# A tile table with 16 segments in the second round; the results of the first seven batches combined during the expert tiles

## The reference

```
h = layernorm(x) * (1 + ca) + sa
x = x + ga * mixer(h)
h = layernorm(x) * (1 + cb) + sb
x = x + gb * moe(h)
```

## Time and profile before

| what | value |
|---|---|
| median of 3 runs | 648.27 us (644.71 to 653.47) |
| the profiled execution | 647.95 us, span 645.8 us |
| busy share of the span | PE 84%, PEld 64%, DVE 75%, ACT 64%, POOL 53% |
| first tile's first layer starts, last tile's | 250.0 us, 587.7 us |
| end stage: first load issued, last ScalarE copy starts | 605.4 us, 642.5 us |
| DMA | 52.23 MB, mean 81 GB/s |

### The profile page before, as it was taken

The page is one execution under the profiler, slowest core; times in us unless marked ns, Lnnn a source line. Parts: engine busy times, 40 slices in busy tenths (PEclk is TensorE's granted clock), DMA queues, the critical chain, the costliest instruction groups (busy, mean ns, idle before and its releaser), DMA issues. The chain is left out here.

```text
span 645.8 us, 15964 instructions
## 1 busy us (share of the span) xinstructions
PE 542.2 (84%) x3102; PEld 411.9 (64%) x3103; DVE 486.6 (75%) x2313; ACT 416.5 (64%) x1126; POOL 341.6 (53%) x442
## 2 busy tenths in 40 slices
PE   2889878886878526978999999999999999997097
PEld 1445444444445414966898888898888898896042
DVE  5989667777577626756898888898888888889187
ACT  0457546555555213756788788888787887887386
POOL 3552656666465654255655655655555656566300
PEclk9999887888888655988999999999999999999589
DMA  6944111111111213121111111111111211110498
GB/s 182 306 151 105 47 41 39 46 42 42 34 47 42 73 39 115 51 55 47 54 58 52 55 53 53 57 53 53 55 51 53 57 47 56 49 51 34 153 369 267
DMA packets 60169, 52.23 MB, mean 81 GB/s; under 512 B 8902, under 2 KB 53177, under 8 KB 60006
## 3 DMA queue, kind: packets, MB, share of 16 engines
q1 hardware_dynamic: 51718, 34.92, 19.5%
q0 software_dynamic: 8416, 16.93, 7.3%
HBM read 29.67 MB, written 22.58 MB: 81 GB/s over the span
## 5 line engine op out<-in xcount | busy, mean ns | idle before, releaser
L493 POOL DMA_INDIRECT expert_rows<-rows,slot x128 | 124.1, 969 | 94.0 <-issue 49.7
L521 POOL DMA_INDIRECT expert_results<-y,target x135 | 134.0, 993 | 49.5 <-issue 48.6
L1190 PE MATMUL bank<-W,h2T 128*128 x1080 | 144.0, 277 | 1.0 <-ACT h2T L626 0.8
L1190 PEld LDWEIGHTS bank<-W,h2T 128*128 128x128 f32 x1080 | 132.4, 193 | 1.7 <-issue 1.7
L618 ACT ACTIVATE h1T<-bank 128x512 f32<-128x512 f32 x135 | 80.4, 596 | 55.4 <-PE bank L1177 49.9
L1006 DVE BATCH_NORM_STATS2 stf<-h1T 128x6 f32<-128x512 f32 x135 | 91.0, 674 | 0.0
L984 DVE SCALAR_TENSOR_TENSOR wmod<-bank,rse,c 128x128 f32<-128x128 f32 x135 | 47.4, 351 | 56.0 <-issue 29.2
L1181 PE MATMUL bank<-ident,h1T 128*128 128x128 f32 x540 | 82.3, 275 | 1.7 <-ACT h1T L618 1.7
L1181 PEld LDWEIGHTS bank<-ident,h1T 128*128 128x128 f32 x540 | 68.4, 143 | 21.4 <-ACT h1T L618 2.5
L626 ACT ACTIVATE h2T<-bank 128x512 f32<-128x512 f32 x135 | 79.1, 586 | 0.3 <-PE bank L1181 0.3
L1174 PE MATMUL bank<-b_parts,onesr 128*128 x135 | 66.1, 489 | 5.5 <-DVE h3lo L998 3.6
(11 more groups left out here) (203 smaller groups left out, 1106.7 us busy)
## 6 DMA issues: line engine op xcount, KB each, us to landing
hrow<-expert_rows SPq DMA_DIRECT2D x135, 65.0 KB
X<-in_L_attn_x SPq DMA_DIRECT2D x8, 512.0 KB, 7.4
W<-expert_results SPq DMA_DIRECT2D x8, 512.0 KB, 6.4
out_x<-X SPq DMA_DIRECT2D x16, 256.0 KB, 5.3
expert_results<-y,target POOLq DMA_INDIRECT x135
expert_rows<-rows,slot POOLq DMA_INDIRECT x128
xi<-expert_results SPq DMA_DIRECT2D x4, 512.0 KB, 7.2
b_parts<-expert_results SPq DMA_DIRECT2D x4, 512.0 KB, 7.5
```

Source lines behind the costliest of these rows:

```text
L493: nc.gpsimd.indirect_dma_start(out=rows_d, out_offset=bass.IndirectOffsetOnAxis(ap=slot[q][:, n // TOPK, n % TOPK:n % TOPK + 1], axis=0), ...
L521: nc.gpsimd.indirect_dma_start(out=results_d, out_offset=bass.IndirectOffsetOnAxis(ap=target[n % TURN][:], axis=0), in_=y[k][:], in_offset ...
L1190: ins = mm(acc, rT[q][:, ch * P:(ch + 1) * P], W2[:, bass.ds(e2 * CF + ch, 1), :], start=(ch == 0), stop=(ch == CF - 1))
```

## The change

- ROUND1_BATCHES is 7 instead of 10, so the first round has 48 tiles and the second 87.
- The second round's table has 16 segments instead of 8: first, per expert, the tiles that still hold rows of the first seven batches, then, per expert, all others. The vectors of the table (nt_f, ends, jump, past, hop) are 16 wide; begin_row holds each segment's first row, jump the step between segments. After tile 63 all results of batches 0 to 6 are computed.
- EARLY = 7 batches are combined during the expert tiles, batch b in turn 10 + b (steps 80 to 135). SP loads its results into the two buffers xi (load_early) behind the loads of that turn's tiles, and stores batch b two turns later (store_early). ScalarE does one of its four gate copies at the end of steps n = 3 to 6 (early_y0g), VectorE one of its four sums at the end of steps n = 4 to 7 (early_sum). GpSimd, not VectorE and TensorE, multiplies with gb (ahead of the turn's second tile) and adds to X (ahead of its fifth), both 128x512.
- The early gates are 0.5 + 0.5 tanh(d / 2), from a Tanh ahead of the first Sqrt and two operations of VectorE in step 4. The Sigmoid of the other nine batches stays behind the tiles.
- The loops of turns end at turn 10 on SP, GpSimd, ScalarE and VectorE; turns 10 to 15 are unrolled there. TensorE keeps its loop to turn 16.
- The end stage has nine batches, unrolled on all engines; per batch it does what it did.

```
-    ROUND1_BATCHES = 10
+    ROUND1_BATCHES = 7
...
+        EARLY = ROUND1_BATCHES
+        EARLY_TURN = (ROUND1 + TOPK * E - 1) // 8 + 3
+        early01 = [t[:].rearrange("p c l -> p (c l)").rearrange("p (j k) -> p j k", j=J) for t in xi]
+        early_gb = [t[:, :].rearrange("p (j d) -> p j d", j=J) for t in scan]
...
             peeled(TURN, LOOP2[0])
-            with engine.Fori(LOOP2[0] // TURN, LOOP2[1] // TURN) as turn:
+            with engine.Fori(LOOP2[0] // TURN, loop_end // TURN) as turn:
                 loaded = load(turn * TURN + oldest, TURN + 2)
                 for n in range(TURN):
                     step(turn * TURN + n, n, lambda k: loaded[k - oldest + n])
+            for begin in range(loop_end, LOOP2[1], TURN):
+                peeled(begin, begin + TURN)
             peeled(LOOP2[1], LAST2 + 1)
+
+        def early_batch(s):
+
+            b = s // TURN - EARLY_TURN if isinstance(s, int) else -1
+            return b if 0 <= b < EARLY else None
...
+            def results_of(tiles_stored):
+                for n in range(RESULTS):
+                    sp.wait_ge(results_stored[n], 16 * ((tiles_stored + RESULTS - 1 - n) // RESULTS))
+
+            def load_early(b):
+                if b == 0:
+                    results_of(ROUND1 + TOPK * E - 1)
+                if b >= 2:
+                    sp.wait_ge(early_sum_ready, b - 1)
+                sp.dma_start(early01[b % 2], results_v[:, tiles(b), :]).then_inc(early_loaded[b % 2], 16)
+
+            def store_early(b):
+                sp.wait_ge(early_out_ready, b + 1)
+                sp.dma_start(out_v[:, tiles(b), :], X[:, tiles(b), :]).then_inc(out_stored, 16)
+
+            with sp.Fori(ROUND1 // SLOTS, EARLY_TURN) as turn:
                 for n in range(SLOTS):
                     load_next(turn * SLOTS + n, n)
-            for i in range(EXPERT_TILES // SLOTS * SLOTS, EXPERT_TILES):
-                load_next(i, i % SLOTS)
-
-            for n in range(RESULTS):
-                sp.wait_ge(results_stored[n], 16 * ((EXPERT_TILES + RESULTS - 1 - n) // RESULTS))
+            for turn in range(EARLY_TURN, EARLY_TURN + EARLY + 2):
+                for i in range(turn * SLOTS, min((turn + 1) * SLOTS, EXPERT_TILES)):
+                    load_next(i, i % SLOTS)
+                if turn - EARLY_TURN < EARLY:
+                    load_early(turn - EARLY_TURN)
+                if turn - EARLY_TURN >= 2:
+                    store_early(turn - EARLY_TURN - 2)
+
+            results_of(EXPERT_TILES)
...
+            sp.wait_ge(early_sum_ready, EARLY)
             for n in range(Y_SLOTS):
-                load_results(n, n)
-            with sp.Fori(1, B // Y_SLOTS) as turn:
-                for n in range(Y_SLOTS):
-                    b = turn * Y_SLOTS + n
-                    sp.wait_ge(ysum_ready, b - Y_SLOTS + 1)
-                    load_results(b, n)
-                    store_out(b - Y_SLOTS)
-            for n in range(Y_SLOTS):
-                store_out(B - Y_SLOTS + n)
+                load_results(EARLY + n, n)
+            for m in range(B - EARLY):
+                if m + Y_SLOTS < B - EARLY:
+                    sp.wait_ge(ysum_ready, m + 1)
+                    load_results(EARLY + m + Y_SLOTS, m)
+                store_out(EARLY + m)
...
+            def early_gb_of(b):
+                pool.wait_ge(early_sum_ready, b + 1)
+                if b == 0:
+                    pool.wait_ge(gb_loaded, 16)
+                if b >= 2:
+                    pool.wait_ge(early_out_ready, b - 1)
+                nc.gpsimd.tensor_tensor(early_gb[b % 2], ysum[b % 2][:], gb_rows[:, b:b + 1, :].broadcast_to([P, J, D]),
+                                        ALU.mult).then_inc(early_gb_ready, 1)
+
+            def early_out_of(b):
+                pool.wait_ge(early_gb_ready, b + 1)
+                nc.gpsimd.tensor_tensor(X[:, tiles(b), :], X[:, tiles(b), :], early_gb[b % 2], ALU.add).then_inc(early_out_ready, 1)
+
             def turn_of_results(turn, count, first):
                 _, expert = nc.values_load_multi_w_load_instructions(
                     pool_experts[0:1, bass.ds(turn * TURN, count)], engines=(mybir.EngineType.Pool,), min_val=0,
                     max_val=E - 1, skip_runtime_bounds_check_because="a count of experts, cut off at E - 1")
+                b = early_batch(turn * TURN)
                 for n in range(count):
+                    if b is not None and n == 1:
+                        early_gb_of(b)
+                    if b is not None and n == 4:
+                        early_out_of(b)
...
+            with pool.Fori(1, EARLY_TURN) as turn:
+                turn_of_results(turn, TURN, False)
...
+            act.wait_ge(ids_ready, EARLY)
+            nc.scalar.activation(gate[:, 0, 0:EARLY * J], lead[:, 0:EARLY * J], ACT.Tanh, scale=0.5).then_inc(half_gate_ready, 1)
             nc.scalar.activation(root_of_eps[:], eps[:], ACT.Sqrt)
+
+            def early_y0g(b, j):
+                if b == 0 and j == 0:
+                    act.wait_ge(early_gates_ready, 1)
+                if j == 0:
+                    act.wait_ge(early_loaded[b % 2], b // 2 * 16 + 16)
+                    if b >= 2:
+                        act.wait_ge(early_sum_ready, b - 1)
+                nc.scalar.activation(y0g[b % 2][:, j, :], early01[b % 2][:, j, 0:D], ACT.Copy,
+                                     scale=gate[:, 0, b * J + j:b * J + j + 1]).then_inc(early_y0g_ready, 1)
...
+                b = early_batch(s)
+                if b is not None and 3 <= n < 3 + J:
+                    early_y0g(b, n - 3)
+
+            run_tiles(act, expert_step, loop_end=EARLY_TURN * TURN)
...
+                if parts > E:
+                    vec.tensor_scalar(own_turn[:], own_e[:], float(E), -float(E), ALU.is_ge, ALU.mult)
+                    link(vec.tensor_tensor(own_row[:], own_row[:], begin_row[:, 0:1], ALU.add))
+                    link(vec.tensor_tensor(own_e[:], own_e[:], own_turn[:], ALU.add))
...
+                old, new = slice(0, E), slice(E, EE)
                 dve.wait_ge(count_done, 1)
                 vec.tensor_copy(cnt_i[:], bank[5][:, 0:E]).then_inc(counts_ready, 1)
-                link(vec.tensor_scalar(cnt[:], bank[5][:, 0:E], float(P - 1), None, ALU.add))
+                vec.tensor_scalar(cnt[:, old], cnt1_i[:], float(P - 1), None, ALU.add)
+                link(vec.tensor_scalar(cnt[:, new], bank[5][:, 0:E], float(P - 1), None, ALU.add))
                 link(vec.tensor_copy(nt_i[:], cnt[:]))
                 link(vec.tensor_scalar(nt_i[:], nt_i[:], P.bit_length() - 1, None, ALU.logical_shift_right))
                 link(vec.tensor_copy(full[:], nt_i[:]))
-                vec.tensor_tensor(past[:], done1[:, 1:E + 1], done1[:, 0:E], ALU.subtract)
-                link(vec.tensor_tensor(nt_f[:], full[:], done1[:, 0:E], ALU.subtract))
-                link(vec.tensor_tensor(past[:], past[:], nt_f[:], ALU.subtract))
-                link(vec.tensor_scalar(jump[:], past[:], float(P), float(REGION), ALU.mult, ALU.add))
-                spread_table(done1[:, 0:1])
+                vec.scalar_tensor_tensor(begin_row[:, old], done1[:], float(P), base_e[:], ALU.mult, ALU.add)
+                vec.tensor_tensor(nt_f[:, old], full[:, old], done1[:], ALU.subtract)
+                vec.tensor_tensor(nt_f[:, new], full[:, new], full[:, old], ALU.subtract)
+                link(vec.scalar_tensor_tensor(begin_row[:, new], full[:, old], float(P), base_e[:], ALU.mult, ALU.add))
+                link(vec.tensor_tensor(step_of[:], begin_row[:, 1:EE + 1], begin_row[:, 0:EE], ALU.subtract))
+                link(vec.scalar_tensor_tensor(jump[:], nt_f[:], -float(P), step_of[:], ALU.mult, ALU.add))
+                spread_table(EE)
...
+                b = early_batch(s)
+                if b is not None and 4 <= n < 4 + J:
+                    early_sum(b, n - 4)
...
+                if isinstance(s, int) and s == 4:
+                    early_gates()
...
+            def early_gates():
+                part = slice(0, EARLY * J)
+                dve.wait_ge(half_gate_ready, 1)
+                vec.tensor_scalar(gate[:, 1, part], gate[:, 0, part], -0.5, 0.5, ALU.mult, ALU.add)
+                vec.tensor_scalar(gate[:, 0, part], gate[:, 0, part], 0.5, 0.5, ALU.mult, ALU.add).then_inc(early_gates_ready, 1)
+
+            def early_sum(b, j):
+                dve.wait_ge(early_y0g_ready, b * J + j + 1)
+                if b >= 2 and j == 0:
+                    dve.wait_ge(early_gb_ready, b - 1)
+                ins = vec.scalar_tensor_tensor(ysum[b % 2][:, j, :], early01[b % 2][:, j, D:2 * D],
+                                               gate[:, 1, b * J + j:b * J + j + 1], y0g[b % 2][:, j, :], ALU.mult, ALU.add)
+                if j == J - 1:
+                    ins.then_inc(early_sum_ready, 1)
+
+            run_tiles(dve, expert_step, mybir.EngineType.DVE, dve_experts, -5, EARLY_TURN * TURN)
...
+            def sums(m):
```

(4 more changed lines are left out.)

150 lines of the change are left out of this document (71 added, 79 removed).

## The result

The changed kernel takes 666.81 us (median of 4 runs, 664.65 to 671.08) against 646.49 (4 runs, 644.28 to 653.47) beside it: a ratio of **1.029, 95% interval 1.020 to 1.038**. It is slower, at the edge of 2% by the interval, where 650.5 and "within 2%" were predicted, and 4.8 us above the range. The profiled execution took 664.65 us, span 662.8. (In all that follows medians take every execution of a kernel; ratios leave out those more than 1.5% above its fastest.)

What follows compares the result with a forecast made beforehand. TensorE was taken as the bound, full in the expert tiles with VectorE close behind, and again in the end stage. 647.95 - 12.2 + 3.5 + 7.0 + 4.4 = 650.65, stated as 650.5 us; range 638.5 to 662.

Steps and rivals of the forecast that it cites:

- part 5: The rest (first table's move, Tanh gates, 16 segments, early stores, GpSimd's other operations): put at nothing.
- part 3: Turns 10 to 15: ScalarE waits for the late early load, delaying h3hi, h3lo and TensorE; 7.0 us more (0 to 10).
- Part 1: End stage: seven batches leave it at 1.74 us each, 12.2 us less, TensorE staying the bound.
- Part 2: Last tiles: the seventh early batch adds two 128x512 GpSimd operations of about 1.25 us; 3.5 us more (1.5 to 5).
- Part 4: Early-work turns: VectorE's four sums and the turn boundary, with GpSimd's multiplication, delay TensorE; 4.4 us more (0 to 9).
- lock in full: Rival, early-work turns: each of GpSimd's two operations holds VectorE 1.25 us, 10.5 us more, so 661; chance 0.08.
- hidden: Rival, expert tiles: early work is hidden, load and VectorE costs shrink to 0 to 3 us, 639.3 to 642; chance 0.29.
- Straight-line pauses: Rival, six unrolled turns: one VectorE pause each, 18.6 us with some 5 overlapping other stalls, so 664; chance 0.14.
- The end saves less: Rival, end stage: nine batches run at 2.2 us rather than 1.74, 4 us back, 654.5; chance 0.05.

Runs made afterwards that it cites:

- e13: The changed kernel unchanged, run a third time, on one of the later chips: 591.70 us, 1.010 of the kernel before.
- e2: The changed kernel with each early load issued behind its turn's second tile load, six tile loads earlier: 650.29 us, 0.999 of the kernel before.
- e17: The changed kernel with GpSimd's 128x512 operations cut into four 128x128 ones each, early loads left late: 588.85 us, 1.004 of the kernel before.
- e9: The changed kernel with six early batches, loads six tile loads earlier, first table at the tenth batch, GpSimd's operations in 128x128 pieces: 573.36 us, 0.977 of before.
- e5: The changed kernel unchanged, run once more on the second chip: 663.42 us, 1.023 of the kernel before.
- e3: The kernel before with turns 10 to 15 unrolled on SP, GpSimd, ScalarE and VectorE, no early work: 650.75 us, 0.999 of the kernel before.
- e16: The same kernel as e9, run again on another later chip: 573.72 us, 0.979 of the kernel before.
- e6: The changed kernel with six early batches, loads six tile loads earlier, first table at the tenth batch, GpSimd's operations whole: 643.03 us, 0.989 of before.
- e1: The kernel before with ROUND1_BATCHES = 7 alone, no early work: 656.04 us, 1.011 of the kernel before.
- e14: As e9, but with the first table at the seventh batch as in the changed kernel: 574.65 us, 0.980 of the kernel before.

## Why the prediction was wrong

Predicted was +2.7 us, measured +17.0 in the spans: 14.3 us to find. Two steps failed. The larger is in part 5, "the first table moves from one mixer step to another at the same cost": it was put at nothing, and 11.0 us went ahead of tile 16. The other is the stall of part 3 in the turns behind the first, taken as 1.25 us a turn and measured as 2.13, with a fall of TensorE's clock on top for which no part had a term. On a chip of the later kind, where the first costs nothing, the changed kernel is 5.7 us slower than before (e13) with +2.7 predicted; that this is so near is in part luck, since the end stage, better than summed, pays for some of the stalls.

- **Part 1 (end, -12.2): right.** 1.72 us a batch against 1.74. The stage as a whole is 13.5 shorter (40.4 to 26.9): the first load landed in 3.62 instead of 4.03 us, and the second batch's matmuls ran at the full clock, 0.86 us in the chain where before it was 1.46.
- **Part 2 (GpSimd's tail, +3.5): right in place, a third too high.** The estimate of 1.25 us for 128x512 was 1.30; the last addition came 2.35 us later relative to tile 134. Part of the tail showed up as TensorE's wait in turn 16 instead. End and tail together gave -11.2 where -8.7 was summed, 2.5 too pessimistic.
- **Part 3 (early load, +7.0): mechanism right, mis-sized.** The step named (load behind the eighth tile load, ScalarE, h3hi, h3lo, TensorE) is what rows and e2 show. The first turn was right: 3.22 less 2.38 = 0.84 against 0.7. The five later ones took 2.13 on average (4.15, 4.90, 4.24, 4.66, 4.58 at tile n = 5, less 2.38) against 1.25. Of the 0.9 missing, some 0.45 is the issue, 1.0 later than in the first turn where I had 0.55: the target that releases it is held by GpSimd's addition. With short operations (e17) 0.4 of that 1.0 is still there. Some 0.25 is the landing (4.06 from issue to copy on average, 3.8 taken; in four of the five turns a store of 256 KB goes out beside the load). This stall alone is 11.5 us.
- **Part 4 (VectorE, +4.4): size nearly right, cause wrong.** It was put on the four sums and the turn's boundary (0.65 each). With the load ahead the stretch costs 3.3 (134.0 less 130.7), and e2's turns start 2.78 apart from the tile before, as without the change. What costs is VectorE's hold: 0.25 to 0.4 at n = 4 of a turn, and 2.2 in turn 16 (e2: tile 130 0.75, tile 132 1.41). e9 takes all of it away with the sums still there. The rival "lock in full" had the mechanism and priced it at 10.5 instead of 3.3. It counted each of the two operations; but the multiplications of turns 11 to 15 fall on register loads and on wmod and hold nothing, and VectorE's room takes in most of the 1.2 us by which an addition holds the target. (The 5.4 us of idle VectorE in the rival "hidden" were 6.0 by the earlier trace rows.)
- **Parts 3 and 4 together** are 17.1 us, 11.4 predicted. Over 11.5 + 3.3 there are the boundaries, 2.94 to 3.00 in place of 2.78, since both costs fall on the same turns, some 1.0; and the low clock once, 1.5 (tile 126 starts 3.89 us behind 125). The prediction has no term for the clock.
- **Part 5 (first table "at the same cost"): wrong.** This is the largest error, 11.0 us at nothing. I had looked at the instructions only, and they are the same. Shown is a cost of 4 to 7 us on chips with a disturbed mixer stage and of none elsewhere. The rest of the 11.0 stays open. That stretch scatters, with a standard deviation of 4.3 us between executions of the kernel before, and a profiled execution is one draw; but over all executions of the first comparison the distance is no smaller. The changed kernel's four have tile 16 at 313.3 +- 1.5, and an estimate for the four of before, from their mean time of 647.7 less the 2.1 us between time and span and less 346.2, is 299.3 +- 2.1: 14.0 +- 2.6 us. On the chip of e5 it is 306.9 less 303.1, 3.8 +- 1.5.
- **Straight-line pauses** (0.14): out by e3. **The end saves less** (0.05): out, 1.72 us a batch. **Hidden** (0.29): out, but it is what e9 reaches once the load is ahead and the operations are in pieces.

That GpSimd's operation holds VectorE was shown on short ones in the earlier trace rows. It holds by kind of operation: in the changed kernel wmod (L1060, one of its large inputs from PSUM) started five times within a 128x512 operation of GpSimd and took 0.35 us each time, as ever, while the target with two SBUF inputs was held in all six turns behind the first. The Trainium skill, SBUF — State Buffer, section "Who interferes with whom", says just this of two SBUF inputs; the trace agrees. It also says that the order of issue decides who blocks. By the recorded starts the trace does not bear this out: at 517.09 the target had started 0.21 us ahead of GpSimd's addition, at 607.99 even 0.71, and it was held until the addition's end both times. A recorded start need not be the issue, and both times GpSimd's scatter ahead of the addition was still running, so the order of issue itself stays open.

**A version that beats both kernels** came out, e9 (again as e16): six early batches, loads six tile loads ahead, table at the tenth batch, GpSimd in pieces: 0.977 (0.976 to 0.979) and 0.979 (0.976 to 0.982) of the kernel before. Both ran on chips of the later kind; on the first kind only e6, the same with whole operations, was measured (0.989).

## What to carry to other kernels

When a load is put into a queue, put it where its consumer has a step to spare: an in-order engine that reaches it early stops everything behind it, once per turn, and one place earlier in the queue was worth 13.5 us here. A stall can cost more than its length: behind some of them TensorE ran at half its clock for 3.4 us, so look at the granted clock before a long step is put down to another wait. Long operations of GpSimd beside VectorE should be cut to the size of VectorE's slack, and before pricing them ask which of VectorE's operations with two SBUF inputs falls under them and who waits for it, a DMA queue included. Where one stretch of a kernel scatters by several us, compare stretch by stretch over many executions; one profile against another puts the scatter on the change.

## What was not expected of the hardware

The mixer stage runs at two speeds, whatever the kernel: a step is 9.4 us on the three later chips, and on the first two and in the first comparison 12.1 to 13.1 in the median, with single steps of 8 to 23. Tile 16 starts 65 us later there. From tile 16 on the changed kernel takes 352.2 and 355.3 us on the one kind and 351.6 on the other, and most of the difference is its clock (e5). Each chip was used for one group of runs, one after the other, so that it is the chip and not the hour is not shown. Instructions of VectorE, ScalarE and GpSimd take as long on either in the profiles of the changed kernel. TensorE's granted clock does differ, 0.83 over the mixer steps of its first profile (84 to 222 us) against 0.98 in e13 (65 to 175); TensorE also waits more there, and which of the two comes first is not shown. What is longer beside is the time between dependent instructions. A chain of small VectorE operations (mv, ve, then hv twice) in the changed kernel's first profile,

```profile
119.42 0.17 DVE L963 TENSOR_SCALAR ve<-mv 128x8 f32<-128x8 f32 x1 [1.23 <-DVE mv L955]
...
120.84 0.17 DVE L942 SCALAR_TENSOR_TENSOR hv<-sq,ve 128x8 f32<-128x8 f32 x1 [0.32 <-DVE sq L937]
...
122.96 0.17 DVE L942 SCALAR_TENSOR_TENSOR hv<-sq,ve 128x8 f32<-128x8 f32 x1 [0.97 <-DVE sq L937]
123.00 0.78 ACT L643 ACTIVATE skip<-bank,ga_bout,mod 128x512 f32<-128x512 f32 x1 [5.11 <-remote]
```

and the same chain of the same kernel and step in e13, where the chain has no pause and skip waits 2.06 us for TensorE:

```profile
105.46 0.17 DVE L963 TENSOR_SCALAR ve<-mv 128x8 f32<-128x8 f32 x1
...
106.07 0.17 DVE L942 SCALAR_TENSOR_TENSOR hv<-sq,ve 128x8 f32<-128x8 f32 x1
...
106.70 0.15 DVE L942 SCALAR_TENSOR_TENSOR hv<-sq,ve 128x8 f32<-128x8 f32 x1
...
107.20 0.78 ACT L643 ACTIVATE skip<-bank,ga_bout,mod 128x512 f32<-128x512 f32 x1 [2.06 <-PE bank L1224]
```

Operations for which the profile shows no wait but that for the one before them on their own engine start 0.3 to 1.2 us late. SP shows it too: the eight first tile loads are issued in 7.94 us in e1 and in 3.99 in e14. Why this happens in this stage, on one kind of chip, is open.
